# Token-major scores by 32-row tiles: a smaller high part of K, loads on one queue, set-up work reordered

## The reference

```python
x = x + tanh(g_xattn[0]) * xattn(layernorm(x), ctx, ctx, Wq, bq, Wk, bk, Wv, bv, Wo, bo)
x = x + tanh(g_ffn[0])   * ffn(layernorm(x), w1, b1, w2, b2)

# xattn: q, k, v = projections, split in 16 heads of 32
scores = einsum('bhqd,bhkd->bhqk', q, k) / sqrt(32)
ctx = einsum('bhqk,bhkd->bhqd', softmax(scores), v)      # then @ Wo.T + bo

# ffn: qlinear, exact gelu, qlinear (hidden width 2048), where
def qlinear(x2d, w, b):
    xq, sx = quant_per_tensor(x2d)      # round(x / (max|x| / 127))
    wq, sw = quant_per_tensor(w)
    return (xq @ wq.T + b) * (sw * sx)
```

## Time and profile before

| | us |
|---|---|
| device time of the profiled execution | 627.94 |
| span from first to last instruction in it | 626.2 |
| outside the span | 1.7 |
| TensorE matmuls busy (PE) | 591.7 (94% of the span) |
| weight loads (PEld) | 345.8 (55%) |
| VectorE (DVE) | 484.8 (77%) |
| ScalarE (ACT) | 335.7 (54%) |
| GpSimd (POOL) | 188.5 (30%) |

### The profile page before, as it was taken

The page is one execution under the profiler, slowest core; times in us unless marked ns, Lnnn a source line. Parts: engine busy times, 40 slices in busy tenths (PEclk is TensorE's granted clock), DMA queues, the critical chain, the costliest instruction groups (busy, mean ns, idle before and its releaser), DMA issues. The chain is left out here.

```text
span 626.2 us, 9836 instructions
## 1 busy us (share of the span) xinstructions
PE 591.7 (94%) x3453; PEld 345.8 (55%) x3453; DVE 484.8 (77%) x698; ACT 335.7 (54%) x411; POOL 188.5 (30%) x161
## 2 busy tenths in 40 slices
PE   6999899999998999999989797999999989999997
PEld 6845666556567566565575475444444454444443
DVE  5877878968879788688675785889999788974271
ACT  1535366662642735626327237878776669644440
POOL 3115152542321512423104130000000809803383
PEclk8999899999999999999999899999999999999999
DMA  8913000360100100101001117777776969779765
GB/s 307 407 42 115 0 2 2 107 229 1 68 2 0 68 1 2 69 0 67 0 1 67 69 69 284 293 278 287 284 269 244 424 233 371 297 310 356 242 222 184
DMA packets 37188, 98.20 MB, mean 157 GB/s; under 512 B 2720, under 2 KB 3488, under 8 KB 32544
## 3 DMA queue, kind: packets, MB, share of 16 engines
q1 hardware_dynamic: 35808, 96.36, 41.1%
q10 hardware_dynamic: 1344, 1.37, 0.7%
HBM read 55.77 MB, written 41.94 MB: 156 GB/s over the span
## 5 line engine op out<-in xcount | busy, mean ns | idle before, releaser
L1176 PE MATMUL ps<-h_sb,w_q 128*128 128x512 bf16 (+1 forms) x512 | 115.1, 379 | 2.1 <-ACT h_sb L1209 1.1
L1432 PE MATMUL ps<-w_q,h_q 128*128 128x512 bf16 x448 | 96.9, 379 | 0.0
L1176 PEld LDWEIGHTS ps<-h_sb,w_q 128*128 128x128 bf16 x512 | 48.9, 98 | 57.1 <-issue 2.5
L1010 POOL TENSOR_TENSOR c_lo<-c_sb,c_hi 128x512 fp32r<-128x512 f32 x32 | 41.3, 1301 | 121.5 <-ACT c_hi L581 121.5
L1514 POOL TENSOR_TENSOR xo<-xo,b2s 128x512 f32<-128x512 f32 x32 | 56.4, 1794 | 63.7 <-DMA xo<-x_dram 45.2
L1432 PEld LDWEIGHTS ps<-w_q,h_q 128*128 128x128 bf16 x448 | 43.8, 98 | 52.9
L1224 ACT ACTIVATE xo<-ps,b1s,sc 128x1024 f32<-128x1024 f32 x48 | 57.8, 1205 | 18.6 <-PE ps L1176 17.1
L568 ACT ACTIVATE prob<-ps 77x1024 f32<-77x1024 f32 x64 | 61.6, 1012 | 8.9 <-PE ps L378 8.9
L1296 DVE TENSOR_REDUCE hmax<-xo 128x1024 f32 (+1 forms) x48 | 57.2, 1213 | 9.8 <-ACT xo L1224 9.8
L616 ACT ACTIVATE q_hi<-ps,bq_sb 128x512 fp32r<-128x512 f32 x32 | 22.0, 688 | 78.0 <-PE ps L336 77.9
L1019 POOL TENSOR_TENSOR x<-x,bo_gate 128x512 f32<-128x512 f32 (+1 forms) x32 | 41.0, 1292 | 49.3 <-DVE xn L735 33.4
(11 more groups left out here) (139 smaller groups left out, 1108.4 us busy)
## 6 DMA issues: line engine op xcount, KB each, us to landing
h_dram<-xo SPq DMA_DIRECT2D x48, 512.0 KB, 2.7
h_sb<-h_dram SPq DMA_DIRECT2D x16, 1024.0 KB, 11.4
x_dram<-x SPq DMA_DIRECT2D x8, 1024.0 KB, 3.9
xo<-x_dram SPq DMA_DIRECT2D x8, 1024.0 KB, 4.9
x<-h_dram SPq DMA_DIRECT2D x8, 1024.0 KB, 8.2
x<-in_x SPq DMA_DIRECT2D x7, 1024.0 KB, 5.4
out<-xo SPq DMA_DIRECT2D x7, 1024.0 KB, 7.4
x<-in_w_t SPq DMA_DIRECT2D x1, 4096.0 KB, 20.6
```

The source lines that it names most:

```text
L1010: nc.gpsimd.tensor_tensor(c_lo[:, g, :], c_sb[:, g, :], c_hi[:, g, :].bitcast(F32), ALU.subtract).then_inc(c_lo_on, 1)
L1176: mm = nc.tensor.matmul(ps[:, 2 * (m % 2) + s, :], w1_q[:, k, m * P:(m + 1) * P], xq_t[:, one(2 * j + s), k, :], start=(k == 0), stop=(k = ...
L1432: mm = nc.tensor.matmul(ps[:, 4 * s + t, :], h_q[:, s, m, t * P:(t + 1) * P], w2_q[:, m, :], start=(m == 0), stop=(m == MF - 1))
```

## The change

The high part of K becomes one block of 78 columns for each group (`NKE = NK + 1`; the 78th column is zero), in the layout of `k_lo`. `scores_by_token` does each head in its own 32-row tile: 16 matmuls of 78 columns in place of 4 of 308, each head in its own bank, the four token tiles side by side in it. `split_k` becomes one copy and one subtraction. Beside that: the K loads move from ACT's queue to SP's, behind the x tiles; the DVE's identity casts and its clearing of `v` move behind `split_k(0)`; `stats1(1)` in step 0 moves ahead of `q_low(0, 0)`; a POOL memset moves into step 0; 16 idle turns of step 1 go; `w1_max(2)` and `w1_max(3)` move back; three transposes instead of two stand before `project_k(0)`; the idle turns at the end become 40.

```diff
-            sh.k_hi = sb("k_hi", [P, HEADS, NK], F32R)
+            sh.k_hi = sb("k_hi", [P, GROUPS, NKE], F32R)
...
                 for t in range(TT):
                     sp.dma_start(x1[:, t, :], x_v[0][:, t, :]).then_inc(x0_in[t], 16)
+                sp.dma_start(ctx_sb, slices(ctx_t)).then_inc(k_in, 16)
+                sp.dma_start(bk_sb[:], bk).then_inc(k_in, 16)
+                sp.dma_start(sh.bq[:], bq).then_inc(k_in, 16)
+                sp.dma_start(wk_raw, slices(wk_t)).then_inc(k_in, 16)
                 for k in range(KD):
                     sp.dma_start(wq_raw[:, k, :], slices(wq_t)[:, k, :]).then_inc(wq_in[k], 16)
...
                 def scores_by_token(c, m):
+                    if is_step(c, 0) and m == 0:
+                        pe.wait_ge(k_zeroed, 1)
...
                     for t in range(TT):
-                        mm = nc.tensor.matmul(ps[:, t, 0:4 * NK], q_hi[:, m, t * P:(t + 1) * P],
-                                              k_hi[:, 4 * m:4 * m + 4, :].rearrange("p h n -> p (h n)"),
-                                              start=True, stop=True)
-                    mm.then_inc(smax_mm, 1)
+                        for r in range(4):
+                            rows = slice(DK * r, DK * (r + 1))
+                            mm = nc.tensor.matmul(ps[:, r, t * NKE:(t + 1) * NKE], q_hi[rows, m, t * P:(t + 1) * P],
+                                                  k_hi[rows, m, :], start=True, stop=True)
+                            if t == TT - 1 and r % 2:
+                                mm.then_inc(smax_mm, 1)
...
-                        idle_turns(nc, sh, BC, 36)
+                        idle_turns(nc, sh, BC, 40)
...
-                    if is_step(i, 1):
-                        pe.wait_ge(q_lo_on, KD * i + KD)
-                        idle_turns(nc, sh, W1, 16)
                     scores_by_key(i, 1)
...
-                transposes(0, 0)
-                transposes(0, 1)
+                for t in range(TT - 1):
+                    transposes(0, t)
                 project_k(0)
-                transposes(0, 2)
-                transposes(0, 3)
+                transposes(0, TT - 1)
...
-                    for r in range(4):
-                        hi = k_hi[DK * r:DK * (r + 1), :, :].rearrange("p (g r) n -> p g r n", r=4)[:, :, r, :]
-                        nc.scalar.copy(hi, sh.k_t[DK * r:DK * (r + 1), :, b * NK:(b + 1) * NK]).then_inc(k_split_hi, 1)
+                    nc.scalar.copy(k_hi[:, :, 0:NK], sh.k_t[:, :, b * NK:(b + 1) * NK]).then_inc(k_split_hi, 1)
...
-                nc.scalar.dma_start(wk_raw, wk_t.rearrange("(k p) n -> p k n", p=P)).then_inc(k_in, 16)
-                nc.scalar.dma_start(ctx_sb, ctx_t.rearrange("(k p) n -> p k n", p=P)).then_inc(k_in, 16)
-                nc.scalar.dma_start(bk_sb[:], bk).then_inc(k_in, 16)
-                nc.scalar.dma_start(sh.bq[:], bq).then_inc(k_in, 16)
...
-                    for r in range(4):
-                        dve.wait_ge(k_split_hi, 4 * b + r + 1)
-                        q = slice(DK * r, DK * (r + 1))
-                        hi = k_hi[q, :, :].bitcast(F32).rearrange("p (g r) n -> p g r n", r=4)[:, :, r, :]
-                        last = nc.vector.tensor_tensor(k_lo[q, :, :], sh.k_t[q, :, b * NK:(b + 1) * NK], hi, ALU.subtract)
-                    last.then_inc(k_split, 1)
+                    dve.wait_ge(k_split_hi, b + 1)
+                    nc.vector.tensor_tensor(k_lo[:, :, :], sh.k_t[:, :, b * NK:(b + 1) * NK], k_hi[:, :, 0:NK].bitcast(F32),
+                                            ALU.subtract).then_inc(k_split, 1)
...
                 def token_max(c, m):
-                    dve.wait_ge(smax_mm, KD * c + m + 1)
+                    dve.wait_ge(smax_mm, 2 * (KD * c + m) + 2)
...
-                                            ps[:, 0:TT, 0:4 * NK].rearrange("p t (h n) -> p t h n", n=NK),
+                                            ps[:, 0:4, 0:TT * NKE].rearrange("p r (t n) -> p t r n", n=NKE)[:, :, :, 0:NK],
...
+                    if first:
+                        stats1(1)
                     q_low(i, 0)
                     if prev:
                         reciprocals(i - 1)
                     if first:
-                        stats1(1)
                         dve.wait_ge(max_zeroed, 1)
                     token_max(i, 0)
...
-                    if is_step(i, 1):
-                        w1_max(2)
                     if nxt:
                         xt_low(i + 1, 2)
                     if first:
                         w1_max(0)
                     if is_step(i, 1):
-                        w1_max(3)
+                        w1_max(2)
...
                     if first:
                         w1_max(1)
                     if is_step(i, 1):
+                        w1_max(3)
                         dve.wait_ge(w1max_on, KD)
...
-                nc.vector.memset(v[64:P, :, :], 0.0).then_inc(v_padded, 1)
-                dve.wait_ge(ident_in, 16)
-                nc.vector.tensor_copy(sh.ident_b[:], sh.ident[:])
-                for r in range(4):
-                    q = slice(DK * r, DK * (r + 1))
-                    nc.vector.tensor_copy(sh.pick[q, :], sh.ident[q, DK * r:DK * r + GROUPS]).then_inc(idents_on, 1)
                 first_stats(0)
...
                 split_k(0)
+                dve.wait_ge(ident_in, 16)
+                nc.vector.tensor_copy(sh.ident_b[:], sh.ident[:])
+                for r in range(4):
+                    q = slice(DK * r, DK * (r + 1))
+                    nc.vector.tensor_copy(sh.pick[q, :], sh.ident[q, DK * r:DK * r + GROUPS]).then_inc(idents_on, 1)
+                nc.vector.memset(v[64:P, :, :], 0.0).then_inc(v_padded, 1)
                 steps(dve, body)
...
-                nc.gpsimd.memset(k_hi[:, :, :].bitcast(F32), 0.0).then_inc(k_zeroed, 1)
+                nc.gpsimd.memset(k_hi[:, :, NK:NKE].bitcast(F32), 0.0).then_inc(k_zeroed, 1)
```

More of the change, by code:

```diff
@@ L31 @@
 NK = 77
+NKE = NK + 1
 F = 2048
@@ L371, in scores_by_key @@
                             rows = slice(DK * r, DK * (r + 1))
-                            nc.tensor.matmul(ps[0:NK, r, :], k[rows, g if k is k_lo else 4 * g + r, :], q[rows, g, :],
+                            nc.tensor.matmul(ps[0:NK, r, :], k[rows, g, 0:NK], q[rows, g, :],
                                              start=(k is k_hi and q is q_hi), stop=False)
@@ L549, in split_k @@
                         act.wait_ge(k_biased, GROUPS)
-                        act.wait_ge(k_zeroed, 1)
-                    for r in range(4):
-                        hi = k_hi[DK * r:DK * (r + 1), :, :].rearrange("p (g r) n -> p g r n", r=4)[:, :, r, :]
-                        nc.scalar.copy(hi, sh.k_t[DK * r:DK * (r + 1), :, b * NK:(b + 1) * NK]).then_inc(k_split_hi, 1)
+                    nc.scalar.copy(k_hi[:, :, 0:NK], sh.k_t[:, :, b * NK:(b + 1) * NK]).then_inc(k_split_hi, 1)
                 def xt_high(c, t):
@@ L1029, in body @@
                         rstd_1(i + 1)
+                    if is_step(i, 0):
+                        pool.wait_ge(w_lo_on, KD)
+                        pool.wait_ge(ln1_rstd, 3)
+                        nc.gpsimd.memset(prob[64:P, 2:4, :], 0.0).then_inc(prob_padded, 1)
+                        pool.wait_ge(prob_padded, 2)
                     if is_step(i, 2):
@@ L1063, in _ @@
                     nc.gpsimd.tensor_tensor(rstd1[:, t2], ve1[:, t2], minus_half[:, t2], ALU.pow).then_inc(ln1_rstd, 1)
-                pool.wait_ge(w_lo_on, KD)
-                pool.wait_ge(ln1_rstd, 2)
-                nc.gpsimd.memset(prob[64:P, 2:4, :], 0.0).then_inc(prob_padded, 1)
-                pool.wait_ge(prob_padded, 2)
                 steps(pool, body)
```

## The result

The changed kernel takes 634.48 us (median of 4 runs, 633.90 to 638.75) against 626.6 us before: ratio 1.0136, 95% interval 1.009 to 1.0182, so 7.9 us slower. The forecast was +1.9. The direction was right, the size was not.

A forecast was written before the change was run, and what follows sets the result against it. TensorE and its waits were taken as the bound. Groups +3.3, start -2.4, idle turns -0.5, `w1_max(3)` +2.0, `split_k(1)` -0.5 gave +1.9 us: 629.8 against the profiled 627.94, or 628.5 on the median; range 624.5 to 635.0 us.

The forecast's parts named there:

- Part 2: Start of the kernel: x lands earlier, so token scores 1 start at 25.7 or 27.3 us; gain taken as 2.4 us.
- rival C: Clock stays at half speed at the start and longer in step 1: +3.9 us, 630.5 us; chance 0.18.
- Part 1: Token scores: a tiled group takes 0.79 us instead of 0.57, 0.22 more, +3.3 us in all.
- Rival A: Small token-score matmuls bound by streaming or issue, not loads: group 0.99 us, +7.3 us, 633.9 us; chance 0.25.
- Rival B: Entering and leaving tiled token-score blocks is free, groups 0.13 us cheaper: -3.8 us, 622.8 us; chance 0.12.
- Counting 15 groups: Token scores: groups 1 to 3 of step 0, two each in six later steps count: 15 x 0.22 = +3.3 us.
- Part 3, `w1_max(3)`: Step 2: moved behind `amax2`, it makes TensorE wait for a maximum, +1.6 to +2.3 us; +2.0 taken.
- Part 3, idle turns: Step 1: without the 16 turns the key scores start sooner, 1.06 us to gain, less for the clock; -0.5 us taken.
- Part 4: Step 4: the shorter `split_k(1)` saves the DVE 1.4 us, removing TensorE's 0.55 us wait: -0.5 us.
- Part 5: End: four more idle turns still finish before the DVE does: 0 us.
- POOL's clearing: Step 0: the memset on POOL stands before exponentials that come 15 us later: costs nothing.

The follow-up runs named there:

- e7: Kernel before with only the K loads on SP's queue behind the x tiles and three transposes ahead of `project_k(0)`, DVE order kept: 623.50 us, ratio 0.9966.
- e4: Changed kernel with `w1_max(2)` and `w1_max(3)` back at their old places: 632.86 us, ratio 1.0107.
- e6: Changed kernel with the 16 idle turns of step 1 restored: 635.01 us, ratio 1.0142.
- e13: e10 plus the DVE's new start order (casts and clearing behind `split_k(0)`, `stats1(1)` ahead of `q_low(0, 0)`): 632.20 us, ratio 1.0096.
- e9: Changed kernel with the DVE's old start order (casts and clearing ahead of the first statistics, `q_low(0, 0)` first): 634.21 us, ratio 1.0111.
- e1: Kernel before with only the token scores in 32-row tiles and the smaller K split: 630.04 us, ratio 1.0057.
- e10: e7 with the tiled token scores of e1: 628.09 us, ratio 1.0035.
- e15: e10 plus only the change's new places of `w1_max(2)` and `w1_max(3)`: 632.39 us, ratio 1.0094.
- e11: e7 without the 16 idle turns of step 1: 624.66 us, ratio 0.997.
- e16: Changed kernel with the DVE's start order, POOL's clearing and `w1_max` at their old places: 629.78 us, ratio 1.0057.
- e12: e7 with the idle turns of step 1 split, 7 and 9, into two waits for maxima: 624.13 us, ratio 0.9961.
- e8: Kernel before with 78 instead of 308 columns in each full-height token-score matmul, other heads' maxima left out: 623.88 us, ratio 0.9951.
- e14: e10 plus only POOL's clearing of `prob` moved into step 0: 628.60 us, ratio 1.0045.

## Why the prediction was right or wrong

Right in direction, wrong in size, by two steps.

**The step that failed: Part 2.** It forecast token scores 1 at 25.7 to 27.3 us, a gain of 2.4. The order of loads does give that: e7 starts them at 25.22 and gains 2.1 us by the ratio, 2.8 by the medians. In the changed kernel two things take it away. First, `wk` was forecast to land at 10.2, and `project_k` to be done by 15.6 to 17.2; TensorE had `wk` at 12.36 and was done at 18.93. In 15 profiles with the loads behind x TensorE waited for it between 0.33 and 2.55 us; in the four with more than 2 us, and in one with 1.45 (but not in those with 1.44, 1.54 and 1.65), the clock halved during `project_k`, and group 0 started at 23.8 to 24.8 us instead of 21.3 to 22.8. Second, the DVE's new order. `q_low` starts 4.7 us behind the end of `k_lo` in the changed kernel (25.02 - 20.34), and 0.2 us behind it in e7. The forecast had that length: 7.3 us from the end of `project_k` to q-projection 2, and it took 6.9. What it left out shows where `wk` came sooner. In e4, e6 and e13 the same way took 8.2 us, since `k_t` waits for the DVE's `wq_lo`, which is in no term (e13: `project_k` done at 16.87):

```profile
14.98 2.49 DVE L691 TENSOR_TENSOR wq_lo<-prob,wq_hi 128x512 fp32r<-128x512 f32 x4
17.38 1.23 DVE L968 TENSOR_SCALAR k_t<-ps,bk_sb 128x154 f32<-128x154 f32 x4
```

And the wait of 2 us that TensorE then has was followed by half clock in e4 and e13, where token scores 1 came 4.5 us behind q-projection 2 instead of the forecast 2.8; in e6 the clock held and it was 3.0. e13 shows the order alone: +3.8 us. e9 shows, in one profile, that with a late `wk` undoing the order doesn't bring the gain back. The two overlap, and so do their prices.

**The step that was left out: the clock in steps 2 to 7.** The prediction took it as unchanged there; rival C changed it at the start and in step 1 only. T(1-c) grew from 4.6 to 11.4 us, 6.8 of the 9.1 us between the means (5.7 of 8.2 without the run of 638.75 us), as an upper bound. In the profiles three stretches in steps 2, 4 and 6 are new; those in steps 4 and 6 cost 1.2 to 1.3 us each. T less T(1-c) grew by 2.3, near the forecast's +1.9, but that is luck: the start gave 0.2 us in place of 2.4, and the groups cost less than was added up for them. T(1-c) grows with each part that adds a wait or tiled groups: tiled scores +3.1 on the kernel before (e1) and +3.0 on e7 (e10), DVE order +2.3 (e13), `w1_max` +3.0 (e15), turns gone +1.3 (e11) to +3.4 (e16).

The Trainium skill, "TensorE: Matmul & The Clock Gate", in "HAM oscillation — how this bites in real kernels", says that TensorE's waits can bring the clock back to half, again and again. The traces agree for waits (2.04 us in e13, 2.02 in e12, half clock at the end of each), and this was the rule to weigh in Part 2. The same page of the Trainium skill, in "Part 4: PE-mode transpose", says that transposes do not count as activity in the way of matmuls. Here the idle turns are transposes, and kernels that have them show less half clock than those without (mean c 0.9945 in e7 against 0.9925 in e11, 0.9898 in e10 against 0.9845 in e16); in e12 the clock held through two waits that they filled, where it fell in e7. That speaks against the rule, but no run here sets turns against matmuls in the same place, so it stays open. That 32-row matmuls hold the clock worse stands by e1 against e8; whether it is the tiles themselves or the draining around them, these two do not separate.

Point by point:
- Part 1, a group costs 0.79 us: right (0.77), and e1, e8 and e10 agree. Rival A at 633.9 us came nearest in time, by luck: its group of 0.99 us isn't there. Of the Trainium skill's two rules, the draining in "TensorEngine Tiling (Array Packing)", Key Properties, agrees (0.33 us in place of 0.24), and the 62 ns in "Wait - 56ns, not 53.3ns?" are not seen: 16 matmuls pass in about 0.46 us (0.57 less the 0.11 behind them), 29 ns each. Rival B is refuted by the same rows.
- Counting 15 groups: somewhat high. Steps 5 and 6 cost +0.3 each instead of +0.44, since what group 2 and 3 gave back was taken as nothing. By e10 against e7, without their clock stretches, all groups with `split_k` cost about 1.3 us up to group 3 of step 7, where 3.3 - 0.5 was forecast.
- Part 3, `w1_max(3)`: +1.5 us at group 1 as read (1.6 to 2.3), +2.7 by group 3 (with 0.2 of group costs), -1.6 when undone (e4). Right as a wait, too low with the clock if e15 (+3.7) is taken as it stands.
- Part 3, idle turns: -0.4 us from group 1.3 to 2.0, forecast -0.5. That was read from two profiles that both had a half clock of 6.8 us there. The profiles of e11 and e16 took 1.5 and 3.0 us longer there than those of e7 and e10, with the clock at half for 10.2 and 13.7 us; that of e9, without turns and with 3.4 us, took no longer (31.54). In the times it is +0.3 (e11) to +1.4 (e16): the sign of the step was wrong, if anything.
- Part 4: right, group 1 of step 4 follows group 0 in 3.57 us instead of 4.08.
- Part 5: right, nothing.
- POOL's clearing, taken as nothing: +0.6 by the ratio of e14, not told from none, though its profile shows the contention.

What stays open: why a wait behind 32-row matmuls brings the clock down more often than the same wait behind full-height ones, and why `w1_max` costs more on e10 (+3.7) than it gives back in the changed kernel (-1.6). The parts do not add up either: loads, tiles, DVE order, clearing, `w1_max` and turns, each by its own ratio, come to +11.7 us, and the change is +8.5. Why `wk` lands when it does was not tested. The runs of one kernel spread by 1 to 5 us, so the small terms are known to about 1 us only.

## What to carry to other kernels

Read the granted clock as a term of the sum, not as a background: a stretch of half clock cost 1.2 to 1.3 us in a steady step here, and the changed kernel's profile has three new ones, so each edit is to be asked which wait of TensorE it adds or uncovers. Price an early start by what each engine does next: the loads were worth some 2 us as long as the DVE served TensorE's first waits first, and nothing once it first did other work that seemed free. When several edits go in together, add them to a base one at a time; here the loads alone beat both kernels, and the whole lost 7.9 us.

## What the runs showed of the hardware

- Matmuls of 32 rows keep the clock worse than full-height ones of as many columns: mean c 0.9877 (e1, 7 runs) against 0.9932 (e8, 10 runs), with the same order of work around them; three stretches of half clock in steps 2 to 7 of the one profile, one in the other.
- The 1 MB load of `wk`, behind the x tiles on one queue, landed 6.2 to 8.2 us after its issue in kernels with the same order of loads; on the second queue it took 6.1.
- Beside a clearing on POOL (25.85 to 27.66 us in e14) a DVE normalisation of 512 columns took three times its time (0.54 to 1.70 us), and 1.11 us in the changed kernel.
- 16 matmuls of 78 columns in four tiles take 0.46 us, 0.115 for a round of four, and a full-height matmul of 78 columns takes 0.11 too (e8: four in 0.44 us). At the rate of the 512-column ones 78 columns would take 0.04, so the columns do not set it. The prediction's weight load of 128 columns (0.11) fits; no run sets it apart.
